# A two-layer vision block on one core: the lead-in before the first FFN tile put in another order, thirteen steps made fifteen

## What is computed

```python
# layer 0: y = x + attention(norm(x))
value, query = dwconv3x3(x, w_v), dwconv3x3(x, w_q)               # stride 1
key, off = dwconv3x3(x, w_k, stride=2), dwconv3x3(x, w_off1, stride=2)
o = gelu(layernorm(off)); pos = tanh(o @ w_off2 + ref)             # 784 points an image
v_sampled = bilinear(value, pos)                                   # gather of 4 corners
out = query @ (key.T @ v_sampled) * scale; y = out @ w_out
# both layers: FFN on every pixel
scores = x @ gate_w + gate_b; probs = softmax(scores); keep the top 2, renormalised
h = gelu(x @ w1[e] + b1[e]); out = sum_e gate[e] * (h @ w2[e] + b2[e])
# layer 1's mixer: 7x7 + 5x3 + 3x5 + 7x1*1x7 + 5x1*1x5 depthwise, folded into one 7x7
```

## Time and profile before

| | us |
|---|---|
| median of 3 runs (lowest, highest) | 1663.65 (1660.79, 1666.19) |
| the profiled execution, its own time | 1665.84 |
| its span in the trace | 1664.0 |
| PE busy | 1482.3 (89% of the span) |
| DVE busy | 918.6 (55%) |
| ACT busy | 734.9 (44%) |
| POOL busy | 251.8 (15%) |
| first FFN matmul (L1059) starts at | 220.62 |

### The profile page before, as it was taken

One profiled execution on the slowest core, in us unless ns is written; L12 is line 12 of the kernel. 1 busy time (PEld: TensorE's weight loads), 2 busy tenths in 40 slices (PEclk: granted clock), 3 DMA queues, 4 the chain that ended last, 5 costly groups with the idle time before them and its releaser, 6 DMA issues.

```text
span 1664.0 us, 20112 instructions
## 1 busy us (share of the span) xinstructions
PE 1482.3 (89%) x6400; PEld 1004.8 (60%) x6400; DVE 918.6 (55%) x2543; ACT 734.9 (44%) x1534; POOL 251.8 (15%) x190
## 2 busy tenths in 40 slices
PE   3785878988779999988889999999999999998998
PEld 2563655555555676655555677667676776665565
DVE  3836869578994554469994543443434443344323
ACT  3732154246442444445442444453535443355443
POOL 2051325011360000011270000010001000000000
PEclk9986878999899999999899999999999999999999
DMA  3342045134334222333153212352145212320211
GB/s 101 61 128 88 26 99 130 56 107 113 81 81 124 61 77 70 87 99 99 44 137 95 84 60 56 100 139 60 44 98 144 64 46 57 85 67 27 76 58 46
DMA packets 169099, 136.29 MB, mean 82 GB/s; under 512 B 115008, under 2 KB 163010, under 8 KB 168610
## 3 DMA queue, kind: packets, MB, share of 16 engines
q1 hardware_dynamic: 164018, 129.74, 28.6%
q0 software_dynamic: 3072, 4.82, 1.2%
q10 hardware_dynamic: 1904, 0.43, 0.1%
HBM read 95.30 MB, written 39.13 MB: 81 GB/s over the span
## 4 chain that ended last, share of the span: by engine, by line
PE 52%; issue 11%; DVE 10%; ACT 5%; POOL 5%; SPq 2%; DMA 2%; ACTq 0%; POOLq 0%; DVEq 0%
PE y_ps L1052 20%; PE at_ps L1197 9%; PE h_ps L1060 5%; PE h_ps L1061 5%; PE h_ps L1059 5%; POOL pix_mem L958 4%; PE at_ps L1117 3%; DVE vq_mem L1375 3%; ACT ln_cen L773 2%; PE lb_ps L1029 2%; PE lg_ps L1042 1%; POOL ln_rstd L945 1%; DVE part L1331 1%; ACT hidden L898 1%; DMA gate_t<-gates_dram 1%
## 5 line engine op out<-in xcount | busy, mean ns | idle before, releaser
L898 ACT ACTIVATE hidden<-h_ps,b 128x448 f32<-128x448 f32 x672 | 424.6, 635 | 725.8 <-PE h_ps L1061 715.2
L1052 PE MATMUL y_ps<-hidden,w 128*96 128x448 f32 x1344 | 638.6, 560 | 33.3 <-ACT hidden L898 26.9
L1059 PE MATMUL h_ps<-xh,w1h 96*128 96x448 f32 x672 | 475.0, 707 | 1.3 <-ACT pix_mem L818 1.3
L1331 DVE SCALAR_TENSOR_TENSOR part<-y_ps,b,gate_t 96x448 f32<-96x448 f32 x224 | 151.8, 678 | 518.1 <-PE y_ps L1052 479.1
L945 POOL TENSOR_TENSOR ln_rstd<-ln_ve,minus_half 112x4 f32<-112x4 f32 x112 | 148.0, 1321 | 1147.1 <-DVE ln_ve L1314 1137.6
L1052 PEld LDWEIGHTS y_ps<-hidden,w 128*96 128x96 f32 x1344 | 206.8, 167 | 108.9 <-ACT hidden L898 66.6
L1060 PE MATMUL h_ps<-xl,w1h 96*128 96x448 f32 x672 | 250.7, 373 | 0.0
L1061 PE MATMUL h_ps<-xh,w1l 96*128 96x448 f32 x672 | 248.8, 370 | 0.0
L1059 PEld LDWEIGHTS h_ps<-xh,w1h 96*128 96x128 f32 x672 | 130.9, 195 | 140.6 <-issue 123.9
L1060 PEld LDWEIGHTS h_ps<-xl,w1h 96*128 96x128 f32 x672 | 131.8, 196 | 120.9 <-issue 120.0
L773 ACT ACTIVATE ln_cen<-ln_cen,ln_rstd 112x96 f32<-112x96 f32 x448 | 130.2, 363 | 100.0 <-POOL ln_rstd L945 100.0
(11 more groups left out here) (155 smaller groups left out, 1371.3 us busy)
## 6 DMA issues: line engine op xcount, KB each, us to landing
gate_t<-gates_dram SPq DMA_DIRECT2D x112, 336.0 KB
value_pairs<-pix_mem SPq DMA_DIRECT2D x56, 168.0 KB, 3.2
x_mem<-norm_c SPq DMA_DIRECT2D x16, 420.0 KB, 4.3
ln_x<-in_x SPq DMA_DIRECT2D x28, 168.0 KB
res_mem<-in_x SPq DMA_DIRECT2D x4, 1176.0 KB
x_attn<-res_mem SPq DMA_DIRECT2D x16, 294.0 KB, 2.7
res<-x_attn SPq DMA_DIRECT2D x28, 168.0 KB
x_ffn<-ffn_out SPq DMA_DIRECT2D x28, 168.0 KB, 2.0
```

What stands on the lines that cost most here:

```text
L898: act.activation(hidden[c % HID_RING][:, :], h_ps[c % H_BANKS][:, 0:TILE], ACT.Gelu, bias=b1[l][:, c:c + 1]).then_inc(gelu_done, 1)
L1052: pe.matmul(y_ps[e % Y_BANKS][0:C, 0:TILE], w2[l][:, c, :], hidden[c % HID_RING][:, :], start=(j == 0), stop=(j == CPE - 1)).then_inc(hid_ ...
L1059: pe.matmul(ps, hi, xh[:, ring(k)], start=True, stop=False)
L1331: dve.scalar_tensor_tensor(part[:, e, :], y_ps[e % Y_BANKS][0:C, 0:TILE], b2[l][:, e:e + 1], gate_t[e // 2][0:C, e % 2, :], ALU.add, ALU.m ...
```

## The change

The lead-in gets 15 steps for 13, and nearly every table that orders it is rewritten.

1. **Jobs.** Tiles 1 to 3 of image 1 (its tile 0 stands in step 3 as before) move from steps 6 and 7 to steps 4 and 5, ahead of image 0's attention. Two more tiles of image 2 come into the lead-in (24 jobs in it for 22), so that the FFN tiles (0, 1) and (0, 2) have one job each beside them for two. The last two FFN tiles of image 0 and the second half of its gates stay beside FFN tiles (0, 0) and (0, 1).
2. **Two banks** for `turn_in` up to the first FFN job: even jobs in `lt_ps`, odd ones in `lg_ps`. `turn_in` waits for the job before in the same bank. The place-1 tile is turned at chunk 6 for 8 (before `turn_back` of the place-0 tile, not behind it).
3. **Attention.** Image 0's stages stand in steps 5 to 11 (before 4 to 10), image 1's first three in 12 to 14 (before 10 to 12, the first beside image 0's last). Three of image 0's six `query` convolutions and the `key` ones get other places; the eight `times_query` pieces are spread over steps 11 and 12.
4. **Gates, first half.** On DVE they are made before `offsets` of image 1; PE turns them and ACT takes them in step 14, not in FFN tile (0, 0).
5. **Weights.** `expand_w_out` moves from step 8 to step 4, `fold_taps` from 8 to 9, `split_weights(0)` from 9 to 11.
6. **Start.** Four tap loads go from SP's queue to ACT's, an early activation brings the ACT table load forward, and the zero stores of `norm_a` come later on SP.
7. **One added wait**: behind a place-1 job in a step with value taps DVE waits for POOL's power before it goes on to the taps.

The diff, cut to its core:

```diff
-LEAD = 13
+LEAD = 15
 START_JOBS = {(-1, 0): [("a0", 0), ("a0", 1)], (-1, 1): [("a0", 2), ("a0", 3)], (-1, 2): [("a0", 4), ("a0", 5)],
-              (-1, 3): [("a0", 6), ("a1", 0)], (-1, 6): [("a1", 1), ("a1", 2)], (-1, 7): [("a1", 3), ("a1", 4)],
-              (-1, 8): [("a1", 5), ("a1", 6)], (-1, 9): [("a2", 0), ("a2", 1)], (-1, 10): [("a2", 2), ("f0", 0)],
-              (-1, 11): [("f0", 1), ("f0", 2)], (-1, 12): [("f0", 3), ("f0", 4)], (0, 0): [("f0", 5), ("f0", 6)],
-              (0, 1): [("a2", 3), ("a2", 4)], (0, 2): [("a2", 5), ("a2", 6)]}
-START_ATTN = {4: [(0, 0)], 5: [(0, 1)], 6: [(0, 2)], 7: [(0, 3)], 8: [(0, 4)], 9: [(0, 5)], 10: [(1, 0), (0, 6)],
-              11: [(1, 1)], 12: [(1, 2)]}
+              (-1, 3): [("a0", 6), ("a1", 0)], (-1, 4): [("a1", 1), ("a1", 2)], (-1, 5): [("a1", 3)],
+              (-1, 7): [("a1", 4)], (-1, 8): [("a1", 5), ("a1", 6)], (-1, 9): [("a2", 0), ("a2", 1)],
+              (-1, 10): [("a2", 2), ("a2", 3)], (-1, 11): [("a2", 4), ("f0", 0)], (-1, 12): [("f0", 1), ("f0", 2)],
+              (-1, 13): [("f0", 3), ("f0", 4)], (0, 0): [("f0", 5), ("f0", 6)], (0, 1): [("a2", 5)],
+              (0, 2): [None, ("a2", 6)]}
+START_ATTN = {5: [(0, 0)], 6: [(0, 1)], 7: [(0, 2)], 8: [(0, 3)], 9: [(0, 4)], 10: [(0, 5)], 11: [(0, 6)],
+              12: [(1, 0)], 13: [(1, 1)], 14: [(1, 2)]}
+LEAD_Y = {(11, 5): 0, (11, 6): 1, (11, 7): 2, (11, 9): 3, (12, 0): 4, (12, 3): 5, (12, 7): 6, (12, 9): 7}
...
+GATE_TURN[-1, LEAD - 1] = 0, 0
...
+        QUERY_CONV = {(1, 3): (0, 0), (1, 5): (0, 1), (2, 10): (0, 2), (3, 8): (1, 0), (3, 10): (1, 1), (4, 3): (1, 2)}
+        KEY_CONV = {(0, 2, 11): 0, (0, 3, 2): 1, (0, 3, 3): 2, (1, 2, 0): 0, (1, 2, 1): 1, (1, 2, 2): 2}
...
+        def turn_bank(n):
+            return lg_ps if n < first_f and n % 2 else lt_ps
+
+        def same_bank(n):
+            return max([m for m in range(n) if turn_bank(m) is turn_bank(n)], default=-1)
...
+                for dst, src in tap_rows[:4]:
+                    load(dst, src)
+            act.wait_ge(pool_set, 1)
+            act.activation(g_p[0][:, 0, 0:1], zeros[0:SUB, 0:1], ACT.Copy, scale=1.0)
...
-                        if slot < 0 and c == LEAD_APPLY[job.place] or slot >= 0 and c == APPLY and job.place == 0:
+                        if slot < 0 and c == (LEAD_APPLY[job.place] if p != 7 else 8) or slot >= 0 and c == APPLY and job.place == 0:
...
-                if n > 0:
-                    pe.wait_ge(ln_centered, n)
+                if same_bank(n) >= 0:
+                    pe.wait_ge(ln_centered, same_bank(n) + 1)
...
-            BESIDE_LEAD = {(2, "normalize0"): norm_off, (2, "combine1"): apply_off, (2, "combine2"): offsets,
+            BESIDE_LEAD = {(2, "normalize0"): norm_off, (2, "combine1"): apply_off, (2, "scores"): offsets,
...
                     if name == "normalize1" and 1 in jobs:
                         normalize(jobs[1])
+                        if slot < 0 and ops:
+                            dve.wait_ge(ln_scale, jobs[1].n + 1)
...
-                if (slot, p) == (-1, 8):
+                if (slot, p) == (-1, 4):
                     expand_w_out()
+                if (slot, p) == (-1, 9):
                     fold_taps()
```

More of the change, by code:

```diff
@@ L103 @@
              **{(slot, TILES - 2 + part): (slot + 1, part) for slot in range(SLOTS - 1) for part in range(2)}}
-GATE_TURN = {after: GATE_STEP[step] for step, after in zip(STEPS, STEPS[1:]) if step in GATE_STEP}
+GATE_TURN = {after: GATE_STEP[step] for step, after in zip(STEPS, STEPS[1:]) if step in GATE_STEP and after != (0, 0)}
+GATE_TURN[-1, LEAD - 1] = 0, 0
 def ffn_slot(slot):
@@ L424, in norm_stores @@
             return 16 * sum(job.norm == norm and not direct(job) and job.n % 2 == parity and job.tile < tiles for job in PLACED)
+        first_f = next(job.n for job in PLACED if job.kind == "f")
+        def turn_bank(n):
+            return lg_ps if n < first_f and n % 2 else lt_ps
+        def same_bank(n):
+            return max([m for m in range(n) if turn_bank(m) is turn_bank(n)], default=-1)
         def direct(job):
@@ L867, in attention @@
                         take_off(b, ((0, 1), (8, 10))[b].index(c))
[L868 to L869 removed]
+                    if b == 0 and (stage, c) in QUERY_TAKE:
+                        take_conv(b, "query", *QUERY_TAKE[stage, c])
                     if stage == 2 and c == 9:
                         gelu_off(b)
[L872 to L873 removed]
+                    if (b, stage, c) in KEY_TAKE:
+                        take_conv(b, "key", 0, KEY_TAKE[b, stage, c])
                     if stage == 2 and c == (10 if b == 0 else 11):
@@ L1148, in attention @@
                         turn_off(b, ((0, 1), (8, 10))[b].index(c))
-                    if (b, stage) in ((0, 1), (0, 3)) and c in (3, 5, 8):
-                        tap_conv(b, "query", stage // 2, (3, 5, 8).index(c))
-                    if stage == 2 and c in ((10, 10, 11), (0, 1, 2))[b]:
-                        for g in range(G):
-                            if ((10, 10, 11), (0, 1, 2))[b][g] == c:
-                                tap_conv(b, "key", 0, g)
+                    if b == 0 and (stage, c) in QUERY_CONV:
+                        tap_conv(b, "query", *QUERY_CONV[stage, c])
+                    if (b, stage, c) in KEY_CONV:
+                        tap_conv(b, "key", 0, KEY_CONV[b, stage, c])
                 if stage == 2 and TURNS <= c < TURNS + VBLK:
@@ L1218, in _ @@
                     for job in JOBS[slot, p]:
-                        if c == (TURN_IN if slot >= 0 else LEAD_TURN_IN)[job.place]:
+                        if c == (LATE_TURN.get((slot, p), TURN_IN[1]) if job.place else TURN_IN[0]):
                             turn_in(job)
@@ L1644, in _ @@
                             sample_row(b, 1)
-                    if 6 in by_stage:
+                    if slot < 0:
+                        for y in LEAD_ADD.get((p, name), ()):
+                            add_y(0, y)
+                    if (slot, p, name) == (-1, 11, "combine0"):
+                        split_weights(0)
+                    if 6 in by_stage and slot >= 0:
                         for y in Y_BEFORE.get(name, ()):
```

63 lines of the change are left out of this document (29 added, 34 removed).

## The result

The changed kernel takes 1675.34 us in the median (1671.35 to 1677.36), the kernel before 1663.65 us (1660.79 to 1666.19). The ratio is 1.0067, with a 95% interval of 1.0047 to 1.0088: slower by 0.67%, where I forecast faster by 1%. Each of the two was run five times for this. The profiled execution took 1675.34 us around a span of 1673.5 us, against 1664.0 before.

A forecast was written before the change was run, and what follows sets the result against it. PE bounds the kernel from 331.5 us on, no engine for long in the lead-in. Terms -8.0, -1.8, -5, -0.5, -1.6 sum to -16.9, taken as -16: 1663.65 becomes 1647.6 us, range 1639 to 1660.

The forecast's parts named there:

- First tiles: Start of the lead-in: a pair of tiles takes 5.9 us for 8.7, image 0's quarters land near 37 for 43.3.
- DVE ahead of the taps: Before image 0's value taps: output weights and an eleventh job start them at 47.4 for 43.3, +4.1 us.
- Value blocks: Lead-in after image 0's taps: blocks turned at 72.8 for 77.0, -4.2; first gather at 92.1 for 99.0, -6.9 us.
- The rival that I gave for slower: Lead-in: convolutions moved behind the value blocks run at 1.2 GHz, +33 us, giving +17, 1680; chance 0.05.
- Gathers to keys: Lead-in, first gather to keys times values: the latter starts at 139.7 for 148.3, -8.6 us.
- Image 0's last stage and image 1's taps: Later lead-in: taps end at 202.4 for 203.6, -1.2 us; added wait costs twice about 1 us, saves slow powers.
- Last step: End of the lead-in: no jobs, gates' first half before the offsets; first gelu at 220.4 for 228.4, -8.0 us.
- FFN tile (0,0): First FFN tile: `combine` no longer waits for the gates, -1.8 us.
- FFN tile (0,1): Second FFN tile: ACT's wait for POOL's power shrinks, -5 of 7.01 us; one job less, -0.5.
- my rival A: FFN tile (0,1): POOL's gathers, slow beside DVE's taps, set the pace; +5, so 1652.5 us; chance 0.27.
- FFN tile (0,2): Third FFN tile, PE-bound: two turns back and one turn in fall away, -1.6 us, near 38.4 us long.
- Behind it: FFN from tile (0,3) on: taken as unchanged, the same within 2 us.

The follow-up runs named there:

- run 1: Changed kernel, with DVE also waiting for POOL's power behind the place-0 tile ahead of image 0's value taps: ratio 0.9982 to the kernel before.
- run 2: Changed kernel with DVE waiting for POOL's power behind the place-0 tile of every lead-in step with taps ("both waits"): 0.9968 to the kernel before.
- run 3: Changed kernel without the waits it added behind place-1 tiles in lead-in steps with taps: 1.0073 to the kernel before.
- run 8: Kernel of run 2 with the gates' first half again made behind offsets and positions and taken in FFN tile (0,0): 0.9983 to the kernel before.
- Run 5: Changed kernel with one tiny DVE tensor_scalar put among image 0's value taps, no further wait: 1.0000 to the kernel before.
- run 6: Kernel of run 2 with POOL's powers put ahead of gathers beside FFN tiles (0,0) and (0,1): 0.9944 to the kernel before.
- run 10: Kernel of run 6 with ACT's exp of the scores two chunks earlier in the last lead-in step: 1652.21 us, 0.9929 to the kernel before.
- run 4: Kernel before, with DVE waiting for POOL's power behind both places of lead-in steps with taps, nothing else: 0.9994 to the kernel before.
- run 7: Kernel before, with only the POOL order of run 6 and no wait: 0.9997 to the kernel before.
- run 12: Kernel of run 10 with the output weights' copy and ping-pong put behind the gathers again: 0.9942 to the kernel before.

## Why the prediction was wrong, step by step

- *First tiles* and *DVE ahead of the taps*: right. 5.86 us a pair for 5.9, taps at 47.75 for 47.4.
- *Value blocks*: **this step failed.** It has PE reach them at 71 behind one query convolution less, and puts the power right ahead of the taps at nothing; PE reached them at 83.93. ACT stood 13.97 us for that power, with the diagonals for the query convolutions behind it in its queue. I checked the added wait only where the change puts it; the tile ahead of image 0's taps is in place 0, without a wait. I had the price in front of me, 6.16 and 5.93 us against 1.01, and read it as the size of a slow power, not as the length of the run of taps beside it, which I had in the earlier trace rows. Cost: 11.2 us at the first gather (run 1). This was none of my rivals. The rival that I gave for slower, convolutions behind the value blocks at the lower clock, did not happen: keys times values came within a microsecond of the forecast once the power was gone.
- *Gathers to keys*: right in length, 47.3 us from the first gather for 47.6.
- *Image 0's last stage and image 1's taps*: 65.4 us for 62.7. I wrote that the added wait "saves POOL's slow powers". It saves neither; the second slow one is again in place 0 and costs 5.1 us of this stretch where the first is mended (67.4 for 62.3 us, runs 1 and 2). The 2 us that I charged for the wait aren't there either: without it the stretch takes 65.6 us (run 3).
- *Last step*: forecast 18.0 us from image 1's offsets to the first gelu, measured 22.9 after, and 22.8 with both waits. Mis-sized by 4.9. I wrote that the value blocks aren't held by key convolutions any more; three of these still stand ahead of them, and the blocks are turned at 223.78, 7 us behind the start of the statistics. And DVE waits 4.70 us for an exp that stands behind copies in ACT's queue, before it makes gates that the offsets queue behind. With the gates late (run 8) the step takes 20.4 us.
- *FFN tile (0,0)*: better than forecast. The wait for the gates is gone, and from first gelu to end it takes 26.4 us for 32.7 before (forecast 30.9). The 4.5 us are largely the other side of the step ahead: with the gates late (run 8) the tile takes 30.8.
- *FFN tile (0,1)*: **this step failed too**: +3.8 for -5.5. It was my rival A and more. Positions and FFN move together, so POOL's chain from the first gather to the power that ACT needs, 35.3 us after (242.12 to 277.36), is as long as the FFN's way to that place; coming early gains nothing. Without the wait for the gates DVE's taps run beside every group of gathers, which then take 1.83 us in the mean for 1.51 before. Run 5 in the list above shows what stretches an operation of POOL, run 6 that its order in the queue is the cause of the stand. But the term was also too large to be had. With one job less, DVE alone is busy for 26.0 us in this tile (25.99 in the changed kernel, 25.97 in runs 6 and 10), and the forecast left it 24.8; I had 27.75 of 30.30 us in the earlier trace rows and didn't hold it against the sum.
- *FFN tile (0,2)*: 40.08 for a forecast of 38.4. The fewer turns are worth nothing here: 38.4 is reached by runs 4, 6, 7, 10 and 12 with PE's granted clock at 0.99 to 1.00, with and without them. That the number fits in the mended kernels is luck.
- *Behind it*: +0.9, within the 2 us that I allowed.

The sum of the misses, 12.0 at the first gather, -0.3 to the keys, 2.7 to image 1's offsets, 4.9, -4.5, 9.3, 1.7 and 0.9, is 26.7, and from -16.9 to +9.5 it is 26.4. With the first cause alone removed the kernel is 0.2% from the kernel before (0.9982, 0.9965 to 0.9999); with both powers and POOL's order mended it is at -0.6 to -0.7%, that is 9 to 12 us of the 16 forecast. In run 10 the rest lies in one place: (0,0) ends at 251.41, where the forecast has 251.4, and (0,1) takes 30.6 us for 24.8.

Two smaller slips: three pairs at 5.9 us for 8.7 give 8.4 us and not 8.6. And the gathers don't contradict the Trainium skill (SBUF — State Buffer, Who interferes with whom) as I wrote. Its inference is on the writing of descriptors, but a gather also reads its indices from SBUF (`o_idx`), and a GpSimd operation that reads SBUF is what the same section calls blocked. No run here tells the two apart, and the 2 us that I derived from the inference have no ground in a trace.

A gain that ten steps of a schedule hand on is gone when one link breaks, and of the chances only 0.02 stood for a wait that I hadn't seen.

## What to carry to other kernels

When work is moved ahead of a long run of vector operations with two SBUF inputs, look for every small operation of GpSimd that is issued at that time, not only for the one that the change guards, and price it at the length of the run: either let the vector engine wait for it (0.67 us here), or put an operation of another kind into the run. In a queue that mixes long rows of transfers with short operations that other engines wait for, put the short ones first; but it pays only once nothing else holds the same place (runs 6 and 7 are the same edit). A wait guards only if something would have run beside it: check what the engine does next. And before a wait is counted as gained in full, hold the shortened stretch against the busy time of every engine in it: tile (0,1) was forecast shorter than DVE's own work.
